# A three-layer interaction kernel: split products and fixed rows in PSUM, a stacked half tile in layer 0, stacked matmuls over 128 rows

## The chip, the core and the metric

One NeuronCore of one Trainium2 chip. The time is the device time of one execution in microseconds. Three runs of the kernel before gave 661.02, 661.69 and 662.90; the median is 661.69.

## The reference, cut to what matters

```python
e = stack([tbl_f[ids[:, f]] for f in range(39)], axis=1)        # 512 x 39 x 16
x0 = xk = e
for idx, (W, b) in enumerate([(w0, b0), (w1, b1), (w2, b2)]):   # W: 39 x k x 128, k = 39, 64, 64
    z = relu(einsum('bhd,bkd,hks->bsd', x0, xk, W) + b[None, :, None])
    if idx != 2: xk = z[:, :64, :]; direct.append(z[:, 64:, :])
    else: direct.append(z)
logit = sum(concatenate(direct, axis=1), axis=-1)               # 512 x 256
h = relu(concatenate([logit, dense_ctx], axis=1) @ W_top1 + b_top1)
h = relu(h @ W_top2 + b_top2)
y = h @ W_top3
```

Everything is fp32. In layer 0 both factors are the same 39 rows, so only the pairs with h <= k are needed, with the two weights added.

## The kernel before, in words

**Chunks and tiles.** The batch is cut into 16 chunks (C) of 32 samples x 16 dimensions = 512 columns (N). A layer multiplies a replicated row of x0 by a row of xk on each of 128 partitions (VectorE, L406) and contracts the products with the weights on TensorE into the PSUM bank z0, z1 or z2. Layers 1 and 2 have 20 such tiles (39 x 64 products, the last tile with 64 partitions), layer 0 has 7. Tiles go in groups of two. For chunk c the order is layer 1 of c, layer 0 of c + 1, layer 2 of c, so that the 24 groups of BODY are numbered 0 to 9 (layer 1), 10 to 13 (layer 0) and 14 to 23 (layer 2).

**Kinds of group** (KINDS, L74). *Whole*, w: fp32 matmuls, each two instructions on TensorE (L528). *Split*, d or p: ScalarE rounds the product to fp32r (high, L639), VectorE (d) or GpSimd (p) subtracts to get the low part (L309), and TensorE makes three fp32r matmuls a tile: high x high (L534), high x low weights (L536), low x high (L539). *Stacked*, h, the last group of layers 1 and 2: its first tile is whole (L519); the second has 64 partitions, whose rounded half (ScalarE, L633) and low half (VectorE, L425) lie one above the other in 128 partitions. One matmul over 128 rows takes both with the high weights (L521), one over 64 rows takes the high half with the low weights (L522).

**What sets the order.** Each engine goes through BODY in order. Products go to a ring of 8 slots in SBUF, high and low parts to rings of 3. VectorE multiplies groups 0 and 1, and 2 and 3, in one instruction of four tiles each (PAIRED, L103) and makes a low part two groups behind its product (LOW_LAG, L105), all that are left before layer 2. The reductions into the logits (L411, L417) stand at fixed groups, as do ScalarE's relus: after_layer1 gives xk1 (L653, L654), without which no product of layer 2 starts; after_layer0 gives xk0 for layer 1 of the next chunk.

**Data.** GpSimd gathers the rows of chunk c + 2 with ten indirect DMAs (L362), all before group 10 (L369). SyncE writes them to DRAM three times over (L266), loads the fixed rows x0_same, in pieces of ANCHORS (L274), and the replicated rows x0_rep in four parts of two DMAs each (L282). Layer 0 reads x0_rep and x0_same, both in SBUF; layers 1 and 2 read x0_rep in SBUF and xk in PSUM. For the first chunk wait_first (L430) waits for the loads.

**Ends.** TensorE starts the dense part of the top layer with three early matmuls in spare banks before chunk 0 (L562) and the fourth behind layer 1 of the last chunk (L580), where the logits of all earlier chunks are added (L573). Then come layer 2 of the last chunk, its logits and two more layers (L597, L603).

Of the kernel before, what the change touches and what calls it, by code (L numbers as in the profile page):

```python
# [41 lines left out]
def pairs_of_layer0():  # L42

    found = {}
    for t in range(T0):
        for p in range(S):
# [42 lines left out]
L0_GROUPS = groups_of(0, T0, [S] * T0)  # L89
# [5 lines left out]
STACKS = [i for i, g in enumerate(BODY) if g[4] == STACKED]  # L95

RING = 8
PART_RING = 3
TURN = -(-len(BODY) // RING) * RING
# [4 lines left out]
assert all(i % 2 == 0 and BODY[i][:1] == BODY[i + 1][:1] and BODY[i][3] == BODY[i + 1][3] for i in PAIRED)  # L104
LOW_LAG = 2  # L105
# [5 lines left out]
    "stacked": lambda g: g[4] == STACKED,  # L111
# [38 lines left out]
def dlrm_cin_kernel(nc, ids, base, tables, dense, w0a, w0b, b0, bx0, w1, b1, bx1, w2, b2,  # L150
# [6 lines left out]
    with ctx:  # L157
# [16 lines left out]
        x0_same = sb("x0_same", [128, 2, N])  # L174
# [7 lines left out]
        w_stack_low = sb("w_stack_low", [HALF, len(STACKS), S], fp32r)  # L182
# [54 lines left out]
        early_loaded = sem("early_loaded")  # L237
# [31 lines left out]
        def load_same(engine, c):  # L269

            for p, n, row in ANCHORS:
                src = x0_rows[bass.ds(c, 1), row:row + 1, 0:N]
                src = bass.AP(src.tensor, src.offset, [[N, n], [1, N]])
                engine.dma_start(x0_same[p:p + n, c % 2, :], src).then_inc(same_loaded, 16)  # L274

        def load_replicated(engine, c, e, part, loaded):

            first, end = part
            src = x0_rows[bass.ds(c, 1), T1 * e + first:T1 * e + first + 1, :]
# [6 lines left out]

        def wait_slot(engine, c, index):
# [476 lines left out]
```

## Time and profile before

| | us |
|---|---|
| median of three runs | 661.69 |
| the profiled execution | 662.2 |
| its span, first to last instruction | 660.4 |
| TensorE busy | 623.2 |
| VectorE busy | 576.9 |
| GpSimd busy | 464.8 |
| ScalarE busy | 283.8 |

In the views PE is TensorE's matmuls, DVE VectorE, ACT ScalarE, POOL GpSimd, SPq SyncE's queue. L12 is line 12 of the kernel. Matmuls are pipelined and their ends modelled: what one costs in a full stream is the distance to the start of the next, or its piece in the chain of waits, not its printed duration. A merged row with x4 lasts from the start of the first to the end of the fourth. A VectorE operation's printed duration overlaps the next one by about 0.08 us. The wait of an instruction held up inside itself is part of its printed duration.

### The profile page before, as it was taken

Reading aid. Unit: us, or ns where it says so; the run is one execution under the profiler, and the core shown is the slowest. Engines: PE = TensorE matmul, PEld = TensorE weight load, DVE = VectorE, ACT = ScalarE, POOL = GpSimd, SP = SyncE. Lnnn points to the kernel's source line nnn. Section 1 sums busy time; section 2 is a strip of 40 time slices with the busy share of each in tenths; the row PEclk is TensorE's granted clock in tenths of the full one; section 3 lists DMA queues with packets and bytes.
Section 4 is the critical chain, followed back from the end, with each engine's and each line's share of the span. In section 5 each row is a group of like instructions: output and inputs, shape, how many; then the busy total and the mean of one; then the engine's idle time right before and its main releaser. Section 6 shows DMA issues by size and latency. Waiting matters only on the chain.

```text
span 660.4 us, 7186 instructions
## 1 busy us (share of the span) xinstructions
PE 623.2 (94%) x1916; PEld 357.3 (54%) x1916; DVE 576.9 (87%) x507; ACT 283.8 (43%) x341; POOL 464.8 (70%) x277
## 2 busy tenths in 40 slices
PE   0359999999999999999999999999999999999998
PEld 0125555555656555555655555555656555555553
DVE  3358899999999999999999999999999999999670
ACT  2123554444344554444344554444344554444223
POOL 6609877786869877786869877786869877706240
PEclk9998999999999999999999999999999999999999
DMA  6789796877949395967949395967949394962000
GB/s 228 168 201 207 148 211 143 191 148 157 194 109 218 69 223 103 202 136 162 190 109 214 70 222 107 201 137 158 194 111 216 75 227 95 201 132 68 2 0 0
DMA packets 28511, 98.20 MB, mean 149 GB/s; under 512 B 8081, under 2 KB 17041, under 8 KB 20434
## 3 DMA queue, kind: packets, MB, share of 16 engines
q1 hardware_dynamic: 21267, 93.54, 64.1%
q0 software_dynamic: 5120, 1.32, 2.0%
q10 hardware_dynamic: 2111, 3.20, 1.4%
q14 instruction: 10, 0.08, 0.0%
q8 instruction: 3, 0.05, 0.0%
HBM read 94.20 MB, written 3.84 MB: 148 GB/s over the span
## 4 chain that ended last, share of the span: by engine, by line
PE 86%; DVE 5%; issue 4%; ACT 1%; DMA 1%; POOL 1%; SPq 1%; DVEq 0%; POOLq 0%; ACTq 0%
PE z L528 40%; PE z L539 13%; PE z L534 12%; PE z L536 11%; PE z L519 4%; DVE products L406 4%; PE z L522 2%; DMA x_rep<-x_rows 1%; POOL low L309 1%; PE z L521 1%; PE spare L573 1%; PE z L597 1%; DVE low L309 1%; PE xk L597 1%; ACT xk L623 1%
## 5 line engine op out<-in xcount | busy, mean ns | idle before, releaser
L406 DVE TENSOR_TENSOR products<-x_rep,xk 128x1024 f32<-128x1024 f32 (+1 forms) x288 | 366.6, 1333 | 25.5 <-ACT xk L623 25.1
L309 POOL TENSOR_TENSOR low<-products,high 128x1024 fp32r<-128x1024 f32 x112 | 264.9, 2390 | 125.3 <-ACT high L639 83.9
L528 PE MATMUL z<-products,w_whole 128*128 128x512 f32 x672 | 311.2, 595 | 0.0
L639 ACT ACTIVATE high<-products 128x1024 fp32r<-128x1024 f32 x176 | 184.3, 1056 | 237.6 <-DVE products L406 180.5
L362 POOL DMA_INDIRECT gathered<-in_tables,rows_sb x160 | 199.1, 1245 | 46.5 <-issue 44.4
L534 PE MATMUL z<-high,w_high 128*128 128x512 f32 x352 | 187.9, 534 | 10.0 <-ACT high L639 10.0
L528 PEld LDWEIGHTS z<-products,w_whole 128*128 128x128 f32 x672 | 128.1, 191 | 112.0 <-issue 99.1
L536 PE MATMUL z<-high,w_low 128*128 128x512 f32 x352 | 139.7, 397 | 0.0
L539 PE MATMUL z<-low,w_high 128*128 128x512 f32 x352 | 113.9, 405 | 3.0 <-DVE low L309 2.3
L534 PEld LDWEIGHTS z<-high,w_high 128*128 128x128 f32 x352 | 66.8, 190 | 55.5 <-issue 32.9
L309 DVE TENSOR_TENSOR low<-products,high 128x1024 fp32r<-128x1024 f32 x64 | 94.2, 1473 | 1.1 <-ACT high L639 1.1
L536 PEld LDWEIGHTS z<-high,w_low 128*128 128x128 f32 x352 | 66.9, 190 | 35.8 <-issue 26.8
L406 DVE TENSOR_TENSOR products<-x_rep,x_same 128x1024 f32 (+1 forms) x64 | 69.3, 1084 | 14.3 <-DMA x_same<-x_rows 10.3
L539 PEld LDWEIGHTS z<-low,w_high 128*128 128x128 f32 x352 | 64.0, 189 | 28.8 <-POOL low L309 12.8
L623 ACT ACTIVATE xk<-z,bx_sb 64x512 f32<-64x512 f32 x64 | 41.7, 651 | 83.9 <-PE z L522 72.1
L425 DVE TENSOR_TENSOR stacks<-products,stacks 64x512 fp32r<-64x512 f32 x32 | 31.7, 991 | 11.9 <-ACT stacks L633 11.4
L623 ACT ACTIVATE direct<-z,b_sb 64x512 f32<-64x512 f32 (+1 forms) x48 | 32.5, 677 | 15.4 <-PE z L522 8.1
L519 PE MATMUL z<-products,w_whole 128*128 128x512 f32 x64 | 32.6, 591 | 0.0
L633 ACT ACTIVATE stacks<-products 64x512 fp32r<-64x512 f32 x32 | 19.9, 623 | 19.2 <-DVE products L406 19.2
L562 PE MATMUL spare<-products 16*128 16x512 f32 x6 | 5.5, 1078 | 21.4 <-DMA x_rows<-gathered 21.4
L521 PE MATMUL z<-stacks,w_stack_high 128*128 128x512 f32 x32 | 25.4, 792 | 0.0
L417 DVE TENSOR_REDUCE logit<-direct 128x512 f32 (+1 forms) x16 | 10.9, 680 | 7.5 <-ACT direct L623 7.5
(34 smaller groups left out, 102.5 us busy)
## 6 DMA issues: line engine op xcount, KB each, us to landing
x_rep<-x_rows SPq DMA_DIRECT2D x60, 768.0 KB
x_rep<-x_rows SPq DMA_DIRECT2D x62, 512.0 KB, 6.4
x_rows<-gathered SPq DMA_DIRECT2D x15, 225.0 KB
x_rep<-x_rows SPq DMA_DIRECT2D x8, 384.0 KB, 16.0
x_rep<-in_w ACTq DMA_DIRECT2D x2, 1280.0 KB
gathered<-in_tables,rows_sb POOLq DMA_INDIRECT x160
x_same<-x_rows SPq DMA_DIRECT2D x15, 90.0 KB
x_same<-x_rows SPq DMA_DIRECT2D x15, 78.0 KB
```

Of the source, the lines that this page charges most:

```text
L309: ops.tensor_tensor(low[0:p, slot, 0:n, :], products[0:p, index % RING, 0:n, :], high[0:p, slot, 0:n, :].bitcast(fp32), ALU.subtract).then ...
L362: pool.indirect_dma_start(out=gathered[:, c % 2, j * D:(j + 1) * D], out_offset=None, in_=tables, in_offset=bass.IndirectOffsetOnAxis(ap=r ...
L406: nc.vector.tensor_tensor(slots, rep, row.unsqueeze(1).broadcast_to([p, n, N]), ALU.mult).then_inc(made, 1 + pair)
L425: nc.vector.tensor_tensor(stacks[HALF:128, at, :], products[0:HALF, index % RING, 1, :], stacks[0:HALF, at, :].bitcast(fp32), ALU.subtract ...
L519: nc.tensor.matmul(out, w_whole[:, at, 0, :], products[:, slot, 0, :], start=False, stop=False)
L521: nc.tensor.matmul(out, w_stack_high[:, stack, :], stacks[:, stack, :], start=False, stop=False)
L528: mm = nc.tensor.matmul(out, w_whole[0:p, at, i, :], products[0:p, slot, i, :], start=(t + i == 0), stop=(t + i == tiles[layer] - 1))
L534: nc.tensor.matmul(out, w_high[0:p, at, i, :], high[0:p, part, i, :], start=(t + i == 0), stop=False)
L536: nc.tensor.matmul(out, w_low[0:p, at, i, :], high[0:p, part, i, :], start=False, stop=False)
L539: mm = nc.tensor.matmul(out, w_high[0:p, at, i, :], low[0:p, part, i, :], start=False, stop=(t + i == tiles[layer] - 1))
L623: return nc.scalar.activation(out, in_, RELU, bias=bias)
L639: nc.scalar.activation(high[0:p, slot, 0:n, :], products[0:p, index % RING, 0:n, :], ACT.Copy).then_inc(rounded, 1)
```

## The change

- **PSUM.** The products of the d groups go to a PSUM pair of banks, d_products, and no longer to the ring; ScalarE and VectorE read them there. The fixed rows are loaded to SBUF once (not double) and copied to a PSUM bank x0_bank by ScalarE (copy_same, behind group 1's rounding); layer 0 reads them there. The three spare banks and the early matmuls go; all four dense matmuls stand behind layer 1 of the last chunk.
- **Kinds.** d groups 4 to 3, p groups 7 to 8 a chunk. Layer 0: its seventh tile has 64 partitions (other ANCHORS, and the second half's rows turned by row_of) and is taken second, alone, split and stacked ("s").
- **Stacks.** The matmul with the low weights runs over all 128 rows.
- **Order.** LOW_LAG is 1, and before a d product all outstanding low parts of VectorE are made. One gather stands behind the low part of group 1 and nine behind that of group 6. after_layer1 comes one group later, after_layer2, after_layer0 and the reduction of L411 one earlier. The waits for loads name exactly the parts that a group reads.

```diff
 T0 = 7
-ANCHORS = [(0, F, 0), (F, 16, 25), (55, 9, 41), (HALF, 16, 6), (80, 3, 22), (83, 45, 32)]
+TURNED = 5
+ANCHORS = [(0, 32, 12), (32, 2, 44), (34, 30, 14), (HALF, 9, 5), (73, 6, 6), (79, F, 1), (118, 10, 31)]
+
+
+def row_of(e, t):
+
+    return T1 + (t + TURNED) % (T1 - 1) if e else t
+
 def field_of(p, t):
-    return (p % HALF + p // HALF * T1 + t) % F
+    return (p % HALF + row_of(p // HALF, t)) % F
...
-def part_of(t):
-
-    return next(q for q, (first, end) in enumerate(PARTS) if first <= t < end)
+assert all(row_of(1, end - 1) - row_of(1, first) == end - 1 - first for first, end in PARTS)
+
+
+def parts_new(index, parts):
+
+    layer, t, n = BODY[index][:3]
+    if index in PAIRED:
+        n += BODY[index + 1][2]
+    before = {u for i in range(STARTS[layer], index) for u in range(BODY[i][1], BODY[i][1] + BODY[i][2])}
+    return [q for q, (first, end) in enumerate(parts)
+            if before.isdisjoint(range(first, end)) and not set(range(t, t + n)).isdisjoint(range(first, end))]
...
-LETTER = {"w": WHOLE, "d": LOW_DVE, "p": LOW_POOL, "h": STACKED}
-KINDS = {1: "pwppwpwddh", 0: "dwww", 2: "wdwpwpwpwh"}
+ALONE = "one tile of 64 partitions, split and stacked"
+LETTER = {"w": WHOLE, "d": LOW_DVE, "p": LOW_POOL, "h": STACKED, "s": ALONE}
+KINDS = {1: "wpwpwppwdh", 0: "wsdw", 2: "wwpwpdpwph"}
...
+        if letter == "s":
+            found.append((layer, tiles - 1, 1, partitions[-1:], ALONE))
+            tiles -= 1
+            continue
...
+RINGED = [i for i, g in enumerate(BODY) if g[4] != LOW_DVE]
 RING = 8
 PART_RING = 3
-TURN = -(-len(BODY) // RING) * RING
+TURN = -(-len(RINGED) // RING) * RING
 PART_TURN = -(-len(SPLIT) // PART_RING) * PART_RING
 WHOLES = [i for i, g in enumerate(BODY) if g[4] in (WHOLE, STACKED)]
 WEIGHT_ORDER = [*LAYER0, *range(N1), *range(N1 + N0, len(BODY))]
 PAIRED = [0,2]
-assert all(i % 2 == 0 and BODY[i][:1] == BODY[i + 1][:1] and BODY[i][3] == BODY[i + 1][3] for i in PAIRED)
-LOW_LAG = 2
+assert all(RINGED.index(i) % 2 == 0 and RINGED.index(i + 1) == RINGED.index(i) + 1 for i in PAIRED)
+assert all(BODY[i][:1] == BODY[i + 1][:1] and BODY[i][3] == BODY[i + 1][3] for i in PAIRED)
+GATHERS = {1: 1, 6: 9}
+assert sum(GATHERS.values()) == GB
+LOW_LAG = 1
...
-        x0_same = sb("x0_same", [128, 2, N])
+        x0_same = sb("x0_same", [128, N])
...
-        w_stack_low = sb("w_stack_low", [HALF, len(STACKS), S], fp32r)
+        w_stack_low = sb("w_stack_low", [S, len(STACKS), S], fp32r)
...
-        early_dense = products[0:DENSE, RING - 1, 0, :]
-        early_wt1d = products[0:DENSE, RING - 1, 1, :]
-        assert all(i % RING != RING - 1 for i in LAYER0)
...
-        spare = [bank("spare0"), bank("spare1"), bank("spare2")]
-        EARLY = len(spare)
-        z_hidden1 = [spare[0], spare[1], spare[2], z[0]]
-        z_hidden2 = [z[1], xk[0]]
+        x0_bank = bank("x0_bank")
+        d_products = ctx.enter_context(nc.psum_tensor("d_products", [128, 2, N], fp32))
+        z_hidden1 = [x0_bank, z[0], xk[0], z[1]]
+        z_hidden2 = [d_products[:, 0, :], d_products[:, 1, :]]
         z_y = xk[1]
...
+        def product(index, p, n):
+
+            if index in RINGED:
+                return products[0:p, RINGED.index(index) % RING, 0:n, :]
+            return d_products[0:p, 0:n, :]
...
+                sent = 0
                 for index in range(len(BODY)):
-                    if index == N1 and c + 2 < C:
-                        gather(c + 2)
                     if BODY[index][4] == LOW_POOL and not (c == C - 1 and index in LAYER0):
                         low_part(pool, nc.gpsimd, c, index)
+                    if index in GATHERS and c + 2 < C:
+                        if sent == 0:
+                            pool.wait_ge(x0_written, 16 * WRITES * (c + 1))
+                        for j in range(sent, sent + GATHERS[index]):
+                            gather(c + 2, j)
+                        sent += GATHERS[index]
...
-                    row = x0_same[0:p, bass.ds(half, 1), :].rearrange("p a n -> p (a n)")
+                    row = x0_bank[0:p, :]
...
+                    if kind == LOW_DVE:
+                        while late:
+                            make_low(c, late.pop(0))
...
-                    if index == N1 + N0 + 4:
+                    if index == N1 + N0 + 3:
...
+                if kind in (STACKED, ALONE):
+                    stack = STACKS.index(index)
+                    if kind == STACKED:
+                        pe.wait_ge(made, count("all", c, index))
+                        nc.tensor.matmul(out, w_whole[:, WHOLES.index(index), 0, :], product(index, 128, 1)[:, 0, :],
+                                         start=False, stop=False)
                     pe.wait_ge(stack_low, count("stacked", c, index))
-                    nc.tensor.matmul(out, w_stack_high[:, stack, :], stacks[:, stack, :], start=False, stop=False)
-                    mm = nc.tensor.matmul(out, w_stack_low[:, stack, :], stacks[0:HALF, stack, :],
-                                          start=False, stop=True)
+                    nc.tensor.matmul(out, w_stack_high[:, stack, :], stacks[:, stack, :], start=first, stop=False)
+                    mm = nc.tensor.matmul(out, w_stack_low[:, stack, :], stacks[:, stack, :],
+                                          start=False, stop=last)
...
-            pe.wait_ge(early_loaded, 32)
-            pe.wait_ge(x0_written, 16 * WRITES)
-            for m in range(EARLY):
-                nc.tensor.matmul(z_hidden1[m][:, :], early_wt1d[:, m * 128:(m + 1) * 128], early_dense,
-                                 start=True, stop=False)
...
-            for m in range(EARLY, H1 // 128):
-                nc.tensor.matmul(z_hidden1[m][:, :], wt1d_sb[:, m * 128:(m + 1) * 128], dense_sb,
-                                 start=True, stop=False)
             pe.wait_ge(logit01_ready, C - 1)
             pe.wait_ge(logit2_ready, C - 1)
             for m in range(H1 // 128):
+                if z_hidden1[m] is z[1]:
+                    pe.wait_ge(direct1_ready, C)
+                nc.tensor.matmul(z_hidden1[m][:, :], wt1d_sb[:, m * 128:(m + 1) * 128], dense_sb,
+                                 start=True, stop=False)
...
+            def copy_same(c):
+
+                act.wait_ge(same_loaded, 16 * len(ANCHORS) * (c + 1))
+                if not (isinstance(c, int) and c == 0):
+                    act.wait_ge(made, count("all", c - 2, N1 + N0 - 1))
+                nc.scalar.activation(x0_bank[:, :], x0_same[:, :], ACT.Copy).then_inc(x0_ready, 1)
...
+                    if index == 2 and not last:
+                        copy_same(c + 1)
+                    if index == 3 and not first:
                         after_layer2(c - 1, first=isinstance(c, int) and c == 1)
-                    if index == N1 + 2:
+                    if index == N1 + 3:
                         after_layer1(c)
-                    if index == N1 + N0 + 4 and not last:
+                    if index == N1 + N0 + 3 and not last:
...
+            copy_same(0)
             for index in LAYER0:
-                if index in SPLIT:
+                if index in SPLIT + STACKS:
...
```

## Rows read from the trace of the kernel before

**Rows 1.** The page: busy time of each engine (share, instructions), and TensorE's granted clock.

```profile
PE 623.2 (94%) x1916; PEld 357.3 (54%) x1916; DVE 576.9 (87%) x507; ACT 283.8 (43%) x341; POOL 464.8 (70%) x277
...
PEclk9998999999999999999999999999999999999999
```

**Rows 2.** Windows view: stretch, length; PE, PEld, DVE, ACT, POOL busy; clock; DMA share, GB/s.

```profile
141.79:178.91 37.12, 37.12 (x118) 21.54 (x117) 35.51 (x31) 17.11 (x21) 29.24 (x17) 1.00 0.75 160
```

**Rows 3.** The chain of waits in order of time: start, us, what.

```profile
67.52 6.01 PE z L528 x14
...
550.38 6.01 PE z L528 x14
```

**Rows 4.** The same chain, closer, in one period: TensorE.

```profile
157.17 0.23 PE z L534
...
158.56 1.72 PE z L528 x4
...
161.36 0.43 PE z L522
161.79 0.43 PE z L534
```

**Rows 5.** Timeline of VectorE in that period: start us, us, engine, line, form [idle before].

```profile
141.74 4.62 DVE L406 TENSOR_TENSOR products<-x_rep,xk 128x1024 f32<-128x1024 f32 x4 [0.81 <-ACT xk L623]
...
149.14 5.73 DVE L406 TENSOR_TENSOR products<-x_rep,xk 128x1024 f32<-128x1024 f32 x5
...
155.57 1.28 DVE L425 TENSOR_TENSOR stacks<-products,stacks 64x512 fp32r<-64x512 f32 x1 [0.70 <-ACT stacks L633]
...
156.88 10.14 DVE L406 TENSOR_TENSOR products<-x_rep,xk 128x2048 f32<-128x2048 f32 x7
...
168.66 2.27 DVE L309 TENSOR_TENSOR low<-products,high 128x1024 fp32r<-128x1024 f32 x1
...
174.37 0.69 DVE L425 TENSOR_TENSOR stacks<-products,stacks 64x512 fp32r<-64x512 f32 x1
```

**Rows 6.** Timeline of GpSimd in that period.

```profile
145.81 0.95 POOL L362 DMA_INDIRECT gathered<-in_tables,rows_sb  x1 [0.31 <-issue]
...
151.58 4.72 POOL L309 TENSOR_TENSOR low<-products,high 128x1024 fp32r<-128x1024 f32 x2 [0.87 <-ACT high L639]
...
160.40 9.45 POOL L309 TENSOR_TENSOR low<-products,high 128x1024 fp32r<-128x1024 f32 x4 [4.10 <-PE z L528]
...
170.00 1.77 POOL L362 DMA_INDIRECT gathered<-in_tables,rows_sb  x1
```

**Rows 7.** Timeline of ScalarE in that period.

```profile
154.90 0.63 ACT L633 ACTIVATE stacks<-products 64x512 fp32r<-64x512 f32 x1 [1.21 <-DVE products L406]
...
159.20 1.06 ACT L639 ACTIVATE high<-products 128x1024 fp32r<-128x1024 f32 x1 [3.67 <-DVE products L406]
...
177.43 1.31 ACT L623 ACTIVATE xk<-z,bx_sb 64x512 f32<-64x512 f32 x2 [4.27 <-PE z L522]
```

**Rows 8.** Groups of instructions by line and form: count, busy us, mean ns, idle before.

```profile
L362 POOL DMA_INDIRECT gathered<-in_tables,rows_sb x160 | 199.1, 1245 | 46.5 <-issue 44.4 <-POOL rows_sb L375 0.3
...
L406 DVE TENSOR_TENSOR products<-x_rep,xk 128x1024 f32<-128x1024 f32 x256 | 296.2, 1214 | 18.8 <-ACT xk L623 18.8
...
L406 DVE TENSOR_TENSOR products<-x_rep,x_same 128x1024 f32 x42 | 51.1, 1217 | 0.4
```

**Rows 9.** Timeline of SyncE's queue in that period: the fixed rows.

```profile
152.42 2.12 SPq L274 DMA_DIRECT2D x_same<-x_rows  x6
```

**Rows 10.** The first chunk: VectorE's timeline, then the chain of waits.

```profile
44.29 11.27 DVE L406 TENSOR_TENSOR products<-x_rep,xk 128x2048 f32<-128x2048 f32 x8 [6.24 <-ACT xk L623]
...
65.51 0.42 PE z L522
```

**Rows 11.** Timeline of TensorE behind layer 1 of the last chunk.

```profile
623.17 1.12 PE L580 MATMUL z<-x_rep 16*128 16x512 f32 x2
624.22 5.10 PE L573 MATMUL spare<-logit,x_rep 128*128 128x480 f32 x12
```

More of the change, by code:

```diff
@@ L45, in pairs_of_layer0 @@
     for t in range(T0):
-        for p in range(S):
+        for p in range(S if t < T0 - 1 else HALF):
             pair = frozenset((anchor_of(p), field_of(p, t)))
@@ L110 @@
     "split": lambda g: g[4] in (LOW_DVE, LOW_POOL),
-    "stacked": lambda g: g[4] == STACKED,
+    "stacked": lambda g: g[4] in (STACKED, ALONE),
     LOW_DVE: lambda g: g[4] == LOW_DVE,
@@ L285, in part_slot @@
             return SPLIT.index(index) % PART_RING
+        def product(index, p, n):
+            if index in RINGED:
+                return products[0:p, RINGED.index(index) % RING, 0:n, :]
+            return d_products[0:p, 0:n, :]
         def wait_slot(engine, c, index):
-            before = before_in_slot(c, index, RING, TURN, range(len(BODY)))
+            if index not in RINGED:
+                earlier = count(LOW_DVE, c, index) - 1
+                if not (isinstance(earlier, int) and earlier == 0):
+                    engine.wait_ge(low_by[LOW_DVE], earlier)
+                return
+            before = before_in_slot(c, RINGED.index(index), RING, TURN, RINGED)
             if before:
                 kind = BODY[before[1]][4]
-                if kind in low_by:
+                if kind == LOW_POOL:
                     engine.wait_ge(low_by[kind], count(kind, *before))
@@ L308, in low_part @@
             slot = part_slot(index)
-            ops.tensor_tensor(low[0:p, slot, 0:n, :], products[0:p, index % RING, 0:n, :],
+            ops.tensor_tensor(low[0:p, slot, 0:n, :], product(index, p, n),
                               high[0:p, slot, 0:n, :].bitcast(fp32), ALU.subtract).then_inc(low_by[kind], 1)
@@ L379, in _ @@
             pool.wait_ge(rows_made, 1)
-            gather(0)
-            gather(1)
+            for c in range(2):
+                for j in range(GB):
+                    gather(c, j)
             for index in LAYER0:
@@ L510, in _ @@
         def _(pe):
-            tiles = [T0, T1, T1]
             def contract(c, index):
                 layer, t, n, partitions, kind = BODY[index]
-                slot, out = index % RING, z[layer][:, :]
-                if kind == STACKED:
-                    at, stack = WHOLES.index(index), STACKS.index(index)
-                    pe.wait_ge(made, count("all", c, index))
-                    nc.tensor.matmul(out, w_whole[:, at, 0, :], products[:, slot, 0, :], start=False, stop=False)
+                out = z[layer][:, :]
+                first, last = index == STARTS[layer], index == ENDS[layer]
+                if kind in (STACKED, ALONE):
[4 more added lines that the diff above has]
+                                         start=False, stop=False)
                     pe.wait_ge(stack_low, count("stacked", c, index))
-                    nc.tensor.matmul(out, w_stack_high[:, stack, :], stacks[:, stack, :], start=False, stop=False)
-                    mm = nc.tensor.matmul(out, w_stack_low[:, stack, :], stacks[0:HALF, stack, :],
-                                          start=False, stop=True)
+                    nc.tensor.matmul(out, w_stack_high[:, stack, :], stacks[:, stack, :], start=first, stop=False)
+                    mm = nc.tensor.matmul(out, w_stack_low[:, stack, :], stacks[:, stack, :],
+                                          start=False, stop=last)
                 elif kind == WHOLE:
@@ L527, in contract @@
                     for i, p in enumerate(partitions):
-                        mm = nc.tensor.matmul(out, w_whole[0:p, at, i, :], products[0:p, slot, i, :],
-                                              start=(t + i == 0), stop=(t + i == tiles[layer] - 1))
+                        mm = nc.tensor.matmul(out, w_whole[0:p, at, i, :], product(index, p, n)[:, i, :],
+                                              start=(first and i == 0), stop=(last and i == n - 1))
                 else:
@@ L534, in contract @@
                         nc.tensor.matmul(out, w_high[0:p, at, i, :], high[0:p, part, i, :],
-                                         start=(t + i == 0), stop=False)
+                                         start=(first and i == 0), stop=False)
                         nc.tensor.matmul(out, w_low[0:p, at, i, :], high[0:p, part, i, :], start=False, stop=False)
@@ L539, in contract @@
                         mm = nc.tensor.matmul(out, w_high[0:p, at, i, :], low[0:p, part, i, :],
-                                              start=False, stop=(t + i == tiles[layer] - 1))
+                                              start=False, stop=(last and i == n - 1))
                 mm.then_inc(used, 1)
```

103 lines of the change are left out of this document (51 added, 52 removed).

## The prediction

> **What bounds the kernel now.** I read the page's busy shares first: TensorE 94%, VectorE 87%, GpSimd 70% of the span, TensorE's clock at full speed but for one slice [rows 1]. One chunk of the steady part, cut out between two starts of layer 2, lasts 37.12 us with TensorE busy throughout and VectorE 35.51 [rows 2]. The chain of waits gives the period more exactly: its 6.01 us piece returns thirteen times from 67.52 to 550.38, so 482.86 / 13 = 37.14 us [rows 3]. Outside the 15 periods lie a start and a tail.
>
> TensorE's prices [rows 4]: a pair of whole tiles 1.72 us (0.86 a tile), a split pair from 157.17 to 158.56 = 1.39. A stacked pair should be 2 x 0.23, but its second matmul, over 64 rows, takes 0.43 and so does the one behind it: 0.20 extra twice. Before, a chunk is 21 whole tiles + 2 of the stacked groups = 23 x 0.859 = 19.75; 11 split pairs x 1.385 = 15.24; 2 x (0.46 + 0.40) = 1.72; in all 36.7, and 0.4 of waits for low parts.
>
> The second resource is the order VectorE, ScalarE, GpSimd, TensorE. From the start of layer 2 VectorE goes through its ten products, one low part and one reduction; the last products end at 154.87; ScalarE rounds the stacked half until 155.53; VectorE's stacked low part starts at 155.57 and ends at 156.85 instead of 156.26, 0.55 behind the end of GpSimd's low part (156.30) [rows 5, 6, 7]. The low part at 168.66 shows the same: 2.27 us, ended about 1.1 behind GpSimd's last one (169.85) [rows 5, 6]. So a VectorE operation whose two inputs are both in SBUF stands still while GpSimd subtracts. The products with the row in PSUM don't: the five from 149.14 take 5.73 together, 1.13 each as the four from 141.74, though three of them lie under GpSimd's low parts [rows 5, 6]. The Trainium skill (SBUF — State Buffer, "Who interferes with whom") says the same, that the pair is an exclusive lock and one SBUF input doesn't take it; the trace agrees, with 1.28 us here against the 0.69 of the free one at 174.37 [rows 5].
>
> **TensorE's sum.** Whole tiles 23 to 22 a chunk (layer 0's seventh becomes a stacked half): 18.89. Split pairs stay 11: 15.24. Stacked pairs 2 to 3, over 128 rows, no change of row count: 3 x 0.46 = 1.38. Sum 35.5, 1.6 less than 37.1. Were TensorE alone, that would be 15 x 1.6 = 24 us.
>
> **VectorE's sum.** One low part fewer (-1.13), one stacked low part more (+0.8: the pair behind one starts 0.03 after its end, 156.85 to 156.88, where products overlap by 0.08, so 0.11 is lost at a change of destination [rows 5]), the three that remain read PSUM and are no longer held. Its stacked low part of layer 0 comes at once behind its product, so it waits for ScalarE: +0.7. In total about what it was, less than TensorE; no bound by itself.
>
> **GpSimd.** 8 low parts x 2.36 = 18.9 and ten gathers. The gathers beside layer 0's two-SBUF-input work take 1.77 where others take 0.95 + 0.31 [rows 6]; with the row in PSUM I take 1.26 for each, 12.6. Sum 31.5 of 37: it fits, but its order matters.
>
> **The loop.** I walk from one start of layer 2 to the next, as differences to the rows shown.
> 1. Layer 2 has the same number of products, low parts and reductions, so its last product again ends at 154.87. Splitting group 19 with a lag of one makes VectorE wait for ScalarE some 0.08.
> 2. Now the group just before the last is no whole one but a GpSimd one. Its product ends 1.13 earlier, at 153.74; ScalarE rounds it to 154.84 (1.06 and 0.03); GpSimd starts 0.14 later (as 160.26 to 160.40 [rows 6, 7]), 154.98, and ends at 157.34. The stacked low part, ready at 155.57, lies under it and ends 0.55 later, 157.89 against 156.85: +1.04. The pair of layer 1 starts at 156.88 + 1.12 = 158.00.
> 3. GpSimd's first low part of layer 1 starts 3.52 behind the pair, as now (156.88 to 160.40): 161.52. Then four low parts, 9.45, and between first and second the one gather that was moved there, 1.26: end 172.23.
> 4. TensorE needs that last one: 0.46 for it, a whole pair 1.72, a split pair 1.39, a whole tile 0.86, a stacked pair 0.46 = 4.89, and 0.05 of latency: the last slot ends at 177.17, its matmul 0.16 later, 177.33. ScalarE starts now at 177.43 [rows 7] and behind that nothing changes, so it starts 0.04 to 0.1 earlier (its 0.04 of latency counted or not).
>
> So the period is 37.1 (37.04 to 37.1): **TensorE's 1.6 us are not gained, they turn into waits for GpSimd's low parts in layer 1.** 15 x -0.04 = -0.6 us. What a product into PSUM costs no row shows. Reading it there costs nothing: 1214 against 1217 ns [rows 8]. Below, nothing (or a few ns gained, ScalarE's input included); above, the 0.11 that VectorE loses where its destination changes, twice. I take nothing, since the read row is the nearest; the upper end is one such product on the loop, 15 x 0.22 = +3.3. The Trainium skill (VectorE: DVE Perf Modes, "The TRN2 errata — SBUF-src ops pay a fixed extra latency per instruction") gives VectorE 120 cycles before the first element from PSUM against 58 from SBUF; by it the one low part on the loop would cost an estimated 0.065 us more, 1 us in all. The rows just cited don't show it for a product.
>
> The last two chunks gather nothing, so 1.26 falls out of step 3 there; TensorE takes over soon, I take -0.9 for both. ScalarE's copy of the fixed rows (0.68) falls into layer 1, where it idles; cover gone, it would delay a rounding by that much. SyncE's seven pieces instead of six cost 0.35 of issue, long before their use.
>
> **Start.** Layer 1 of the first chunk starts at 44.29 on VectorE, and TensorE ends it at 65.93 [rows 10]. The copy adds 0.7 before layer 0 and the exact waits for the loads take away 1.1, so I leave 44.3. By steps 3 and 4 layer 1 ends 3.52 + 9.45 + 1.26 + 4.9 = 19.1 later, 63.4: -2.5; half speed for its first matmuls may leave -1. I take -2.0. The three early matmuls that go lie in idle time and give nothing.
>
> **Tail.** They come back behind layer 1 of the last chunk, on TensorE's path: 16-row matmuls, 1.05 from 623.17 to 624.22 and 0.1 for the change back [rows 11], so 3 x 1.1 = +3.3 (no less than 3 x 0.86, no more than 3 x 1.26). The last layer 2 is 15.1 instead of 15.9: -0.7. Net +2.6.
>
> Sum against the profiled execution, 662.2: - 0.6 - 0.9 - 2.0 + 2.6 = 661.3. It stands 0.5 over the median, so **660.8**. Own range of this case: 657 to 666.
>
> **Rivals.**
> (a) *The stacked low part gets in first.* If the gathers stay slow (their mean over the run is 1.245 [rows 8], 1.55 with the pause, so nine end 2.6 later than I take), GpSimd is late for group 22, the stacked low part goes before it, and VectorE keeps its 1.6 us. Then TensorE bounds: between 35.6 and 36.4 (some waits for late low parts stay), so 15 x 0.7 to 1.5: 639 to 651. For it: the slow gathers are real. Against: they are slow only beside work that leaves SBUF, and at 1.26 each GpSimd is free at 172.23 + 9 x 1.26 + 3 x 2.36 = 190.65, while group 22 is rounded at 154.98 + 37.1 = 192.1: 1.4 us to spare.
> (b) *Slower: the low part of group 19 is held too.* It still reads its rounded part from SBUF. It comes seven products and a reduction after 141.74, 8.6, at 150.3; by the clock just used GpSimd subtracts for groups 16 and 18 from 146.5 to 151.2. 0.9 of hold would shift everything behind: 15 x 0.9 = +13, 674. It decides from about 0.2 us a chunk (+3). Against: products with one SBUF input are never held. By the page of the Trainium skill cited in the first part it isn't held at all.
> (c) *ScalarE waits for the fixed rows.* It now takes them at group 2, about 160 on this chunk's clock, where VectorE took them at 170.9, behind its held low part [rows 5]; their issues end at 154.54 [rows 9]. If they land later than 160, every rounding behind waits. 0.5 us a chunk gives 668. The change's PSUM part would then be no gain but a wait.
>
> **Chances.** The forecast 0.55; (a) 0.27; (b) 0.10; (c) 0.08. About 0.3% (2 us) is what a measurement here can tell from no change, so same is 659.7 to 663.7. Of the forecast's 0.55, 0.14 lies below, 0.28 inside, 0.13 above. Faster 0.14 + 0.27 = 0.41, same 0.28, slower 0.13 + 0.18 = 0.31. The range goes from 641 (most of (a)) to 672 ((c) and the mild end of (b)).
>
> **What would show it.** Right: stacked low parts at layer 2's end near 2.2 us; idle time of TensorE's low-part matmuls (now L539) behind GpSimd of some 1.5 us a chunk; period 37.1; the 64-row matmuls' successors at 0.23; nearly all gathers near 0.95. Wrong: a period near 35.6 with a 0.7 us stacked low part (a); VectorE's split low parts over 1.3 us (b); ScalarE idle before its copy on a DMA (c); products into PSUM over 1.25 us.

## The result and the profile after

The change makes the kernel slower by half a per cent: 665.93 us (median of 7 runs, 663.86 to 667.1) against 662.6 (7 runs of the kernel before beside them, 661.02 to 662.95), ratio 1.0053, 95% interval 1.0041 to 1.0066. The forecast was 660.8, "no change" in size, with 657 to 666 as its own range: the time lies at the very edge of that range, and the sign was missed. The profiled execution took 666.94, its span (first to last instruction) is 665.1.

First the page of the changed kernel, against [rows 1] and [rows 8]: TensorE 14.6 us less busy, ScalarE 19 more, the gathers down from 1245 to 988 ns.

```profile
PE 608.6 (92%) x1916; PEld 358.2 (54%) x1916; DVE 571.7 (86%) x507; ACT 303.2 (46%) x374; POOL 462.2 (69%) x293
...
PEclk9987999999999999999999999999999999999999
...
L391 POOL DMA_INDIRECT gathered<-in_tables,rows_sb x160 | 158.1, 988 | 44.5 <-issue 42.1
```

Its chain of waits, one piece of layer 2, as [rows 3]: (554.89 - 73.19) / 13 = 37.05 us a period, against 37.14, forecast "37.04 to 37.1".

```profile
73.19 5.15 PE z L569 x12
...
554.89 5.15 PE z L569 x12
```

VectorE's timeline in one period, as [rows 5]. The stacked low part takes 2.32 us instead of 1.28, the pair of layer 1 follows it, and the low part made from d_products isn't held. Layer 2 starts at 145.44 in this timeline, so the pair comes 16.24 behind it, forecast 158.00 - 141.74 = 16.26.

```profile
154.01 1.22 DVE L341 TENSOR_TENSOR low<-d_products,high 128x1024 fp32r<-128x1024 f32 x1
...
159.33 2.32 DVE L461 TENSOR_TENSOR stacks<-products,stacks 64x512 fp32r<-64x512 f32 x1 [0.70 <-ACT stacks L667]
161.68 9.01 DVE L442 TENSOR_TENSOR products<-x_rep,xk 128x2048 f32<-128x2048 f32 x6
```

GpSimd's, as [rows 6]: it stood idle for 0.82 us before the low part of group 22, so it got there first, with less to spare than the 1.4 us of the prediction. This low part ends at 161.10, the stacked one 0.55 behind it; then 165.20, 3.52 behind the pair, and 10.60 to the end of the fourth low part (forecast 3.52 and 10.71).

```profile
158.73 2.37 POOL L341 TENSOR_TENSOR low<-products,high 128x1024 fp32r<-128x1024 f32 x1 [0.82 <-ACT high L673]
165.20 2.39 POOL L341 TENSOR_TENSOR low<-products,high 128x1024 fp32r<-128x1024 f32 x1 [4.10 <-ACT high L673]
167.74 0.95 POOL L391 DMA_INDIRECT gathered<-in_tables,rows_sb  x1
168.70 7.10 POOL L341 TENSOR_TENSOR low<-products,high 128x1024 fp32r<-128x1024 f32 x3
```

VectorE's groups by form, for the prices of PSUM: a product written there costs 1221 ns against 1212 into SBUF, a low part that reads it 1219. The low parts of the kernel before, which read SBUF, have a median of 1218 (source view of L309), those of the changed kernel 1217.

```profile
L442 DVE TENSOR_TENSOR products<-x_rep,xk 128x1024 f32<-128x1024 f32 x224 | 261.0, 1212 | 12.6 <-ACT xk L657 12.6
...
L341 DVE TENSOR_TENSOR low<-d_products,high 128x1024 fp32r<-128x1024 f32 x48 | 58.5, 1219 | 5.5 <-ACT high L673 5.1
L442 DVE TENSOR_TENSOR d_products<-x_rep,xk 128x1024 f32<-128x1024 f32 x32 | 39.1, 1221 | 0.0
```

So the steady part did what was forecast. The two spans differ by 4.7 us. The table cuts them where TensorE ends layer 1 of the first and of the last chunk, and shows where the difference arose:

| stretch | before | after | difference | forecast |
|---|---|---|---|---|
| start, to the end of chunk 0's layer 1 | 65.93 | 69.62 | +3.7 | -2.0 |
| 15 periods | 557.24 | 555.10 | -2.1 | -1.5 |
| tail | 37.23 | 40.38 | +3.15 | +2.6 |

**The start.** Two timelines of the changed kernel's first chunk, ScalarE and GpSimd. Layer 1 begins a microsecond earlier than before (43.28 against 44.29). But ScalarE's copy of chunk 1's fixed rows, put ahead of the third rounding, stood 6.56 us until they landed; three roundings follow in a row, and GpSimd idled 4.66 us between its first and second low part.

```profile
45.60 1.06 ACT L673 ACTIVATE high<-products 128x1024 fp32r<-128x1024 f32 x1 [1.70 <-DVE products L442]
53.21 0.60 ACT L681 ACTIVATE x_bank<-x_same 128x512 f32<-128x512 f32 x1 [6.56 <-DMA x_same<-x_rows]
53.75 2.94 ACT L673 ACTIVATE high<-products 128x1024 fp32r<-128x1024 f32 x3
```

```profile
54.87 7.00 POOL L341 TENSOR_TENSOR low<-products,high 128x1024 fp32r<-128x1024 f32 x3 [4.66 <-ACT high L673]
```

The chain of waits of the same chunk shows a second cost: behind that wait the clock granted to TensorE fell to half (windows view: 0.50 from 57.30 to 61.93), and four matmuls of whole tiles took 3.41 us where 1.72 is their time in [rows 4]. A part of this was there before: in the same place the kernel before shows 1.22 and 2.56 where this one shows 1.22 and 3.41.

```profile
54.87 2.38 POOL low L341
...
57.30 1.22 PE z L580 x2
58.52 3.41 PE z L569 x4
61.93 0.43 PE z L575
```

**The tail.** TensorE's timeline behind the last layer 1, against [rows 11]: each dense matmul pair now stands alone between matmuls over 128 rows. Four times 2.86 us is 11.44 (a pair of 1.05 and four logit matmuls of 1.81, chain of waits). Before, there were one pair of 1.05 and 6.64 for the sixteen logit matmuls behind it, 7.69. Each inserted pair thus costs 1.25, not 1.1.

```profile
624.72 1.12 PE L619 MATMUL x_bank<-x_rep 16*128 16x512 f32 x2
625.77 1.88 PE L608 MATMUL x_bank<-logit,x_rep 128*128 128x480 f32 x4
627.58 1.12 PE L619 MATMUL z<-x_rep 16*128 16x512 f32 x2
```

### The profile page after: what moved, and what is told of

It reads as the page before. It is cut to its first block, busy times and chain, and to the rows that moved or that the text cites. A ratio compares the mean times of both kernels' runs of the same rounds, so it can differ in the third digit from the quotient of the medians.

```text
span 665.1 us, 7215 instructions
## 1 busy us (share of the span) xinstructions
PE 608.6 (92%) x1916; PEld 358.2 (54%) x1916; DVE 571.7 (86%) x507; ACT 303.2 (46%) x374; POOL 462.2 (69%) x293
## 4 chain that ended last, share of the span: by engine, by line
PE 55%; DVE 15%; POOL 14%; issue 6%; ACT 5%; DMA 4%; DVEq 1%; SPq 0%; ACTq 0%; POOLq 0%
PE z L569 25%; DVE products L442 13%; POOL low L341 10%; PE z L580 9%; PE z L575 7%; PE z L577 7%; POOL gathered L391 4%; ACT high L673 3%; PE z L559 2%; DMA x_same<-x_rows 1%; PE d_products L633 1%; DVE d_products L442 1%; PE z L563 1%; PE z L562 1%; ACT xk L657 1%
## 5 line engine op out<-in xcount | busy, mean ns | idle before, releaser
L341 POOL TENSOR_TENSOR low<-products,high 128x1024 fp32r<-128x1024 f32 x128 | 303.4, 2389 | 138.3 <-ACT high L673 137.8
L442 DVE TENSOR_TENSOR products<-x_rep,xk 128x1024 f32<-128x1024 f32 (+1 forms) x256 | 331.4, 1346 | 17.2 <-ACT xk L657 16.7
L673 ACT ACTIVATE high<-products 128x1024 fp32r<-128x1024 f32 x128 | 135.2, 1058 | 187.6 <-DVE products L442 170.9
L391 POOL DMA_INDIRECT gathered<-in_tables,rows_sb x160 | 158.1, 988 | 44.5 <-issue 42.1
L580 PE MATMUL z<-low,w_high 128*128 128x512 f32 x352 | 114.3, 406 | 13.1 <-POOL low L341 11.3
L580 PEld LDWEIGHTS z<-low,w_high 128*128 128x128 f32 x352 | 63.0, 188 | 42.1 <-POOL low L341 30.4
L461 DVE TENSOR_TENSOR stacks<-products,stacks 64x512 fp32r<-64x512 f32 x48 | 59.3, 1236 | 28.8 <-ACT stacks L667 28.3
L673 ACT ACTIVATE high<-d_products 128x1024 fp32r<-128x1024 f32 x48 | 49.2, 1025 | 52.5 <-DVE d_products L442 31.0
L341 DVE TENSOR_TENSOR low<-d_products,high 128x1024 fp32r<-128x1024 f32 x48 | 58.5, 1219 | 5.5 <-ACT high L673 5.1
L442 DVE TENSOR_TENSOR products<-x_rep,x_bank 128x1024 f32<-128x1024 f32 (+1 forms) x48 | 49.6, 1036 | 15.6 <-ACT x_bank L681 13.8
L442 DVE TENSOR_TENSOR d_products<-x_rep,xk 128x1024 f32<-128x1024 f32 x32 | 39.1, 1221 | 0.0
L562 PE MATMUL z<-stacks,w_stack_high 128*128 128x512 f32 x48 | 38.7, 806 | 0.0
```

Source lines behind the costliest of these rows:

```text
L341: ops.tensor_tensor(low[0:p, slot, 0:n, :], product(index, p, n), high[0:p, slot, 0:n, :].bitcast(fp32), ALU.subtract).then_inc(low_by[kin ...
L391: pool.indirect_dma_start(out=gathered[:, c % 2, j * D:(j + 1) * D], out_offset=None, in_=tables, in_offset=bass.IndirectOffsetOnAxis(ap=r ...
L442: nc.vector.tensor_tensor(slots, rep, row.unsqueeze(1).broadcast_to([p, n, N]), ALU.mult).then_inc(made, 1 + pair)
L461: nc.vector.tensor_tensor(stacks[HALF:128, at, :], product(index, HALF, BODY[index][2])[:, BODY[index][2] - 1, :], stacks[0:HALF, at, :].b ...
L562: nc.tensor.matmul(out, w_stack_high[:, stack, :], stacks[:, stack, :], start=first, stop=False)
L580: mm = nc.tensor.matmul(out, w_high[0:p, at, i, :], low[0:p, part, i, :], start=False, stop=(last and i == n - 1))
```

## Experiments

Ratios are to the kernel before, run on the same chip. Where an edit adds lines above TensorE's part, its line numbers are shifted by six.

### The copy of chunk 1's fixed rows made later

```diff
-                    if index == 2 and not last:
+                    if index == (8 if first else 2) and not last:
                         copy_same(c + 1)
```

> ScalarE copies the fixed rows of chunk 1 behind group 6 of chunk 0 instead of behind group 1; all later chunks as in the change. Theory A (the start is lost because ScalarE's copy waits 6.6 us for its load and holds back the rounding of groups 3, 5 and 6): that wait goes, TensorE ends layer 1 of chunk 0 near 64 to 66 instead of 69.6, the period stays 37.0, the time falls by 3.5 to 5 us, to 661 to 662.5. Rival B (the start is lost to the late first product, 32.4 us, and to TensorE's half clock): less than 1 us is won.

Measured: 665.87 us, ratio 1.0064 (1.0048 to 1.008): no gain. Yet the wait is gone, and TensorE ends chunk 0's layer 1 at 63.6, 6.0 us earlier, near the 63.4 of the prediction. Two things took it back. VectorE's timeline shows the first: layer 0 now came before chunk 1's replicated rows, whose loads SyncE issues behind those of the fixed rows. The longer of the two waits, 2.80 us, stands before the seventh tile. The change takes this tile second, so it asks for the second part of the rows one group earlier than the kernel before, where VectorE waited 0.46 for it and went on at 62.97.

```profile
58.28 1.22 DVE L442 TENSOR_TENSOR products<-x_rep,x_bank 128x1024 f32<-128x1024 f32 x1 [1.19 <-DMA x_rep<-x_rows]
...
63.02 0.68 DVE L442 TENSOR_TENSOR products<-x_rep,x_bank 64x512 f32<-64x512 f32 x1 [2.80 <-DMA x_rep<-x_rows]
```

Of 6.0 us there were 2.4 left at the second chunk, and 2.1 at the last (chain of waits; the changed kernel has 110.39 and 591.35):

```profile
108.02 5.15 PE z L569 x12
...
589.22 5.15 PE z L569 x12
...
651.88 8.80 PE d_products L633 x16
```

The last row is the second: these sixteen matmuls of the top layers took 7.13 us in the changed kernel. The window view of them has the clock at 0.81 of full speed, with the same work and no wait inside. That accounts for the profiled execution; for the medians it is only argued, from the mean granted clock of the runs (0.990 to 0.997 here, 0.992 to 0.997 in the changed kernel).

```profile
651.88:660.68 8.80, 8.80 (x17) 3.67 (x18) 0.00 (x0) 2.37 (x4) 0.00 (x0) 0.81 0.00 0
```

### The stacked low part behind the next chunk's first pair

```diff
+                carried = not (isinstance(c, int) and c <= 0)
+                passed = not (isinstance(c, int) and c in (-1, C - 1))
...
+                    if index == 0 and carried:
+                        make_low(c - 1, len(BODY) - 1)
...
+                if passed:
+                    assert late.pop() == len(BODY) - 1
                 for index in late:
                     make_low(c, index)
```

> The stacked low part at the end of layer 2 is made by VectorE behind the first pair of the next chunk's layer 1, not before it. Theory A (the loop layer 2, held stacked low part, first pair, GpSimd's low parts sets the period): the 0.70 us wait and the 1.6 us hold leave the loop, the period falls from 37.0 to TensorE's own 35.5 to 35.9, the time by 15 to 22 us, to 644 to 651. Rival B (GpSimd's rate sets it, 8 low parts and 10 gathers, whatever the stacked low part does): period 36.8 to 37.1, less than 3 us won.

Measured: 642.79 us, ratio 0.9718 (0.9698 to 0.9737). The period is (568.39 - 71.67) / 14 = 35.48, which is the prediction's sum for TensorE alone, 35.5. VectorE's groups have the stacked low parts at 766 ns instead of 1236.

```profile
71.67 5.15 PE z L575 x12
...
568.39 5.15 PE z L575 x12
```

```profile
L461 DVE TENSOR_TENSOR stacks<-products,stacks 64x512 fp32r<-64x512 f32 x48 | 36.8, 766 | 18.7 <-ACT stacks L673 17.7
```

So the wait and the hold of the stacked low part at the end of layer 2 held the loop, and the 1.6 us a chunk that the change takes off TensorE lay behind them.

### The same move in the kernel before

The edit is the same as above, made in the kernel before.

> The kernel before, with one edit of the same kind: the stacked low part of its last group is made behind the first pair of the next chunk. Theory: the change's lighter TensorE (35.5 against 36.7 us a chunk by the prediction's sums) and the free loop are both needed for 642.8; here TensorE's own 36.7 sets the period, so 15 x 0.3 to 0.45 is all there is to gain: 654 to 658 us, ratio 0.989 to 0.994. Rival: the gain of 23 us was all in the place of the stacked low part and has nothing to do with the change: 640 to 646, ratio about 0.97.

Measured: 655.74 us, ratio 0.9901 (0.9886 to 0.9916), period (581.51 - 67.80) / 14 = 36.69, the prediction's 36.7.

```profile
67.80 6.01 PE z L534 x14
...
581.51 6.01 PE z L534 x14
```

The move alone is worth 6 us (661.97 to 655.74), the change on top of it another 13; without the move the change costs 3.

### The matmul with the low weights over 64 rows again

```diff
-w_stack_low[:, stack, :], stacks[:, stack, :],
+w_stack_low[0:HALF, stack, :], stacks[0:HALF, stack, :],
```

> The matmul with the low weights goes over 64 rows again, in all three stacked groups; the rest as in the change. TensorE alone would pay 3 x 0.40 = 1.2 us a chunk, 18 us. Theory A (TensorE has 1.5 us of waits a chunk, so most of it is hidden; only what lies behind the low part of group 6 counts): 0.2 to 0.5 us a chunk, 3 to 8 us slower than the change. Rival B (TensorE bounds): 15 to 18 us slower, 681 to 684.

Measured: 673.39 us, ratio 1.0174 (1.0153 to 1.0195), 7.5 over the change; period 37.63, 0.58 more. In time this is theory A; a chunk costs slightly more than its 0.5. The part of the change that uses 128 rows is a gain even where TensorE doesn't set the period; the prediction's step 4 has a stacked pair on the loop. How the 0.58 splits over the three stacked pairs wasn't separated.

### VectorE's split products back in SBUF

```diff
-RINGED = [i for i, g in enumerate(BODY) if g[4] != LOW_DVE]
+RINGED = list(range(len(BODY)))
...
-                if kind == LOW_POOL:
+                if kind in low_by:
```

> The change, with VectorE's three split products a chunk put back into the ring in SBUF, all else as it is. Theory: VectorE's low parts then read two inputs from SBUF and are held while GpSimd subtracts; the one in layer 2 (group 19) lies on the loop, held by up to 0.9 us, so the period rises from 37.05 to 37.3 at least and 38.0 at most: 669 to 681 us, ratio 1.012 to 1.03, and those low parts average over 1.4 us. Rival: they fall where GpSimd pauses and aren't held, or the hold is hidden by the hold of the stacked low part behind them: 665 to 667.

Measured: 715.87 us, ratio 1.08 (1.078 to 1.082), over three times the most that was expected (715.87 - 665.93 = 50, against 15). VectorE's timeline, then GpSimd's: the low part of group 19 takes 2.58 us, the one at 141.03 3.43, 2381 ns on average, and it is mutual: GpSimd's take 5.74 for two.

```profile
141.03 3.43 DVE L341 TENSOR_TENSOR low<-products,high 128x1024 fp32r<-128x1024 f32 x1
...
160.68 2.58 DVE L341 TENSOR_TENSOR low<-products,high 128x1024 fp32r<-128x1024 f32 x1
```

```profile
159.79 5.74 POOL L341 TENSOR_TENSOR low<-products,high 128x1024 fp32r<-128x1024 f32 x2 [0.61 <-ACT high L673]
```

With eight low parts on GpSimd, VectorE's own must not have two inputs in SBUF: this part of the change carries the others. It is not quite that part alone: with these products the ring's eight slots serve 24 groups a chunk again instead of 21. VectorE waited for TensorE, which frees most slots, only 0.2 us in the whole run. It is rival (b) with the cover taken away; the prediction priced one such hold at 13 us, and all three with what they do to GpSimd cost 50.

### The fixed rows back in SBUF

The copy and its semaphore go, x0_same has two halves, and layer 0 reads them, as in the kernel before.

> The change, with the fixed rows of layer 0 read from SBUF in two halves as in the kernel before, so no copy by ScalarE. Theory A: some four of the nine gathers behind group 6 are held again by layer 0's work (1.77 against 0.95 us), GpSimd comes 2 to 3 us later to group 22, the stacked low part of group 23 gets in before it (mean near 0.7 to 0.9 us) and the period falls to 35.7 to 36.7: 643 to 660 us. Theory B: the order stays as in the change, the period stays near 37.05, and only the wait of the copy in the start goes: 662 to 665. Theory C: GpSimd's lateness is carried into the next chunk's layer 1 and costs more than the order brings: above 668.

Measured: 677.72 us, ratio 1.023 (1.0213 to 1.0247): theory C. Part of the gathers are held while layer 0's products run, as the chain of waits shows. Since the last gather must go before the low part at 150.62, the loop now runs over them; one period is 38.08 (150.62 to 188.70). So this part of the change, the copy to PSUM, is worth 12 us (677.72 - 665.93).

```profile
137.41 1.76 POOL gathered L391
...
140.90 2.21 POOL gathered L391
...
150.62 2.41 POOL low L341
```

VectorE is held too: a product of layer 0 took 2.29 us (136.05) where it takes 1.21, beside a low part of GpSimd that ended at 137.25.

### The gathers spread

GATHERS = {6: 8, 16: 1, 20: 1} in place of {1: 1, 6: 9}.

> The ten gathers stand behind the low parts of groups 6 (eight), 16 (one) and 20 (one) instead of 1 (one) and 6 (nine); nothing else. Theory A: the low part of group 22 then starts later than VectorE's stacked low part, which is no longer held (0.7 instead of 2.3 us), and the gather leaves the chain of layer 1: period 35.5 to 36.2, the time falls by 12 to 20 us. Rival B (the hold does not set the period, or the stacked low part stays held): within 3 us of the change, 663 to 667.

Measured: 686.14 us, ratio 1.0373 (1.0353 to 1.0393); neither theory had that. The period rose to 38.44 (146.50 to 607.76 in the chain of waits, twelve periods), and the stacked low part wasn't freed: at 158.80 it took 3.15 us. The last gather, issued at 158.04, landed at 160.44; only then does SyncE write the rows and load them again, and the chain of waits runs through this:

```profile
160.84 2.27 DMA x_rows<-gathered
...
167.40 10.48 DMA x_rep<-x_rows
```

ScalarE waited for the fixed rows 41.6 us over the run, in all sixteen chunks, 1.5 to 1.7 us each in the four steady ones read; the changed kernel has 21.4, all in the start. VectorE waited for the replicated rows as well (1.14 us before 178.11), and that wait is the one on the chain. So what rival (c) describes can happen in the steady part too: a last gather at 158.04 instead of 149.37 (GpSimd's timelines) is enough. The gathers can't be moved that far back.

### Both edits

> The change with both edits: the fixed rows of chunk 1 copied six groups later (only in chunk 0), and the stacked low part of the last group made behind the first pair of the next chunk. With the second edit alone the run was 642.8 us and TensorE set the period (35.48). Theory: what the late copy saves in the start (2.3 us at the second chunk when it stood alone) was lost at the end only because the loop through GpSimd, and in the profiled run a slower clock of TensorE in the last layer, took it back; with TensorE as the bound it reaches the end: 640.5 to 641.5 us, ratio to the kernel before 0.968 to 0.970. Rival: the wait for the replicated loads that showed up behind the late copy is fixed to the DMA of the start, and nothing is left of the gain: 642.3 to 643.3.

Measured: 641.2 us, ratio 0.9686 (0.9671 to 0.9701), the fastest version found. The second chunk's piece stands at 105.39 against 107.15 without the late copy, the last at 566.62 against 568.39: where TensorE sets the period, what the start saves is kept.

### The dense matmuls grouped

```diff
             for m in range(H1 // 128):
                 nc.tensor.matmul(z_hidden1[m][:, :], wt1d_sb[:, m * 128:(m + 1) * 128], dense_sb,
                                  start=True, stop=False)
+            for m in range(H1 // 128):
                 add_logits(m, 0, logit01, before_last)
```

> The change with the late copy of chunk 1 (alone 665.9 us), and the four dense matmuls of the last part made one after the other before the logits are added. Two things are told apart. First the tail: if the 0.19 us by which a dense matmul pair (1.05) exceeds two of 0.43 is the price of a change of the row count, grouping saves 3 x 0.19 = 0.6 us on TensorE's path. Second the 1.7 us that the late copy's profiled run lost to TensorE's clock in its last 16 matmuls (8.80 instead of 7.13 us): if that fall belongs to that one execution, the time is 661 to 664 us; if it comes back, 665 to 666.

> The version with the late copy and the stacked low part behind the first pair (641.2 us), and the four dense matmuls grouped. Theory: TensorE sets the end of everything here, so the 0.6 us come through: 640.0 to 641.0 us, and the stretch from the first dense matmul to the last logit matmul in front of layer 2 falls from 4 x 2.86 = 11.4 to 10.8 us. Rival: the change of the row count isn't what costs, each pair stays at 1.05: no difference.

In the version with both edits the stretch fell from 11.44 to 10.27 us, more than forecast: the switch of the row count costs 0.19 going in and 0.20 coming back (chain of waits).

```profile
105.43 5.15 PE z L575 x12
...
568.34 5.15 PE z L575 x12
...
600.26 1.05 PE x_bank L625 x2
601.31 0.86 PE z L625 x2
...
603.88 1.81 PE x_bank L614 x4
605.69 1.61 PE z L614 x4
...
628.29 8.83 PE d_products L640 x16
```

But the time was 643.52 us, ratio 0.9718 (0.9691 to 0.9746): no gain, and 2 us more by the medians, though the intervals overlap. Two things took back the 1.17 us in the profiled execution. Its last row is one: the clock fell in the tail, 8.83 us for 7.13, which is 1.7. The other lies in the steady part: its period is (568.34 - 105.43) / 13 = 35.61 against 35.48 in the version without grouping, which makes another 1.7. Why the period rose isn't known; the edit touches nothing there. The five runs order themselves mainly by clock: a mean granted clock of 0.995 for 640.34 and 642.93 us, 0.992 for 643.52, and 0.987 for 644.89 and 644.93. With the late copy alone grouping gave 665.3 us, ratio 1.0045 (1.0032 to 1.0059), and there the clock fell inside the logit matmuls (3.50 us for 1.81):

```profile
624.52 1.71 PE z L619 x2
626.23 3.50 PE x_bank L608 x4
629.72 2.05 PE z L608 x4
```

### Chunk 1's rows written earlier

```diff
+            write_x0(act, 1)
             copy_same(0)
             for index in LAYER0:
                 if index in SPLIT + STACKS:
                     round_high(-1, index)
-            write_x0(act, 1)
```

> The version with the late copy and the stacked low part behind the first pair (641.2 us), and ScalarE issues the write of chunk 1's rows ahead of the copy of chunk 0's fixed rows instead of behind its roundings (it was issued at 37 us and landed at 48.7, and SyncE's loads of chunk 1 wait for it). Theory: the start is bound by when chunk 1's rows are loaded; issued near 32 they land 3 to 5 us earlier, VectorE's waits for the replicated rows in chunk 0's layer 0 (2.09 and 2.77 us) go, ScalarE's copy of chunk 0 comes 0.7 us later: 637.5 to 639.5 us. Rival: the transfers share one bandwidth in the start (DMA busy 99%), so chunk 0's own rows come later by what chunk 1's come earlier: 640.5 to 643.

> The change with only the earlier write of chunk 1's rows. Theory: the wait of ScalarE's copy for the fixed rows in chunk 0 (6.56 us), which is the prediction's missed term, is the lateness of this write; with it 3 to 5 us earlier most of the wait goes, layer 1 of chunk 0 ends on TensorE near 65 instead of 69.6, and layer 0 behind it doesn't wait either: 661 to 663.5 us, no longer slower than the kernel before. Rival: bandwidth, as above, or the loop through GpSimd takes it back: 665 to 667.

Measured: 645.34 us, ratio 0.9745 (0.9731 to 0.9758), with both edits; 668.08, ratio 1.0094 (1.0078 to 1.0109), on the change. Both times the theory and the rival missed. Chunk 1's gathers themselves land only at 36.56, so ScalarE stood for them with the copy of chunk 0 behind it. The chain of waits of the second kernel:

```profile
27.96 8.60 DMA gathered<-in_tables,rows_sb
36.56 0.02 issue
36.58 0.34 ACTq L287
```

Moved forward the write was 1.2 us earlier (36.58 instead of 37.77), and SyncE's loads of the fixed rows began at 47.42 instead of 49.21. With chunk 0's layers all later by some 5.5 us (layer 1 at 48.75 instead of 43.28), ScalarE's copy of chunk 1 no longer waited, which shows once more that its wait depends on when layer 1 comes against these loads. The profiled execution of the first kernel is 5.1 us longer than with both edits alone: 2.1 of it stand at the second chunk (107.45 against 105.39), 1.4 in the thirteen periods up to 570.08 (35.58 each against 35.48), and 1.7 in the last sixteen matmuls (8.83). What would bring the loads earlier stays open.

## Why the prediction was right and wrong

**The loop: right.** The period is 37.05, the stacked low part is held as worked out (2.32 us), TensorE's saved 1.6 us turned into waits. That the place of the stacked low part is the cause is shown by moving it: 35.48. The sign named for it, some 1.5 us a chunk of idle time before the low-part matmuls, is seen only in part: the page has 11.3 us in the whole run before these matmuls and 30.4 before their weight loads. TensorE's two sums, 36.7 and 35.5, came out as the periods of the two kernels where nothing else bounds.

**The prices: right.** Writing to PSUM costs 9 ns at most in the printed means, nothing beside the bound of 0.22 us. That bound came from the 0.11 us lost at a change of destination; in layer 2 VectorE goes from the ring to d_products and back at the usual 1.13 us a product (starts at 150.57, 151.70 and 152.83). The estimate of 0.065 us more for a low part that reads PSUM doesn't show either: 1217 against 1218 ns. Gathers took 988 ns, near 0.95.

**The failing step: the start.** "I take -2.0"; it was +3.7. Against the prediction's 661.3 for the profiled execution, 666.94 is 5.6 too much: 5.7 from the start, 0.55 from the tail, less 0.6 from the periods. The prediction said of ScalarE's copy that it "falls into layer 1, where it idles", and rival (c) looked for its wait only in the steady part. In the first chunk there is no earlier chunk behind which the loads could hide: their issue began at 49.21, behind the write of chunk 1's rows, and the copy stood 6.56 us. The prediction's own walk gives 19.1 us for that layer 1; it took 26.34 (69.62 - 43.28). Some 4.4 of the difference is the wait: the fourth low part ended at 61.87, forecast 43.28 + 14.23 = 57.51. The rest, 2.9, is TensorE at a lower clock behind the wait: 1.22 for 0.46, 3.41 for 1.72, and 0.5 in the three matmuls that follow. With the copy late it ended at 63.6, near the forecast of 63.4, but partly by luck: layer 1 began at 43.22 and not at 44.3, and took 20.4 us and not 19.1, with the clock at 0.69 from 45 to 55. The late copy's run also shows that the wait was not all: chunk 1's replicated rows would have taken back most of a start without it. The forecast of the start had no term for them.

**The tail: right in sign, small in size.** +3.15 against +2.6. The term "3 x 1.1" measured 1.25 each, inside its bound of 1.26: 1.05 for the pair and 0.20 for the change back, where the prediction took 0.1.

**Rivals.** (a) didn't happen: the gathers were fast enough that GpSimd got to group 22 first, with 0.82 us to spare. When the stacked low part was freed by hand the period was 35.48. (b) didn't happen: 1.22 us for the low part of group 19. (c) happened once, in the first chunk. Whether the sign turned on it alone isn't shown: with the wait taken out the time stayed where it was. Where TensorE set the period, taking it out was worth 1.6 us (642.79 to 641.2).

## What to carry to other kernels

Walk the first iteration as an instruction order of its own: what hides behind an earlier iteration in the steady part has nothing to hide behind there, and an operation that waits for a load stalls everything queued behind it on its engine. When a loop through several engines sets the period, find the one operation that can leave it; here a 0.7 us operation moved behind one pair was worth 23 us, six of them in the kernel before as well. Work taken off one engine shows in the time only once that loop is cut.

## What the runs showed of the hardware

- VectorE's operations with two inputs in SBUF and GpSimd's work hold each other, in both directions. With the split products in SBUF, VectorE's low parts took 2381 ns on average instead of 1219, and two of GpSimd's 5.74 us instead of 4.75. With the fixed rows in SBUF, a product took 2.29 us instead of 1.21, and gathers up to 2.21 instead of 0.95.
- The clock granted to TensorE fell in some executions near the end, without a wait ahead that the executions at full clock didn't have too. The sixteen matmuls of the top layers took 8.72 to 8.83 us in seven of the twelve profiled executions of the changed kernel and its variants, and 7.13 in the other five. In the kernel before, all 29 runs that stood beside the experiments had a mean of 0.995; in the changed one it went from 0.992 to 0.997, and its fastest run, 663.86, was the one at 0.997. So 1.7 us come and go between executions of these versions, and a smaller gain can't be told from single ones. What sets it off wasn't found.
- ScalarE rounds 1024 elements in 1025 ns from PSUM and in 1058 from SBUF.
- A change of the row count between matmuls costs about 0.2 us each way: in the tail 1.05 us for a pair over 16 rows behind 128 rows against 0.86 for the next, and 1.81 against 1.61 on the way back.
